# A layer of attention and sixteen experts on one core: five engine programs written anew

## The chip, the cores and the metric

The kernel runs on one core of one Trainium2 chip. TensorE (PE) multiplies, VectorE (DVE), ScalarE (ACT) and GpSimd (POOL) work elementwise, and SyncE (SP) issues the transfers; each follows a program of its own, and they wait for one another on semaphores. The metric is the time of one execution on the device, in microseconds (us); less is better.

## The reference

x has 16 batches of 512 tokens by 256 features, and each batch goes through one layer. What is computed, for a batch:

```
xn  = layernorm(x)
q, gates = split(xn @ Wqg);  k, v = split(xn @ Wkv)     # 16 heads: 16 key and 64 value features each
q, k, v  = q/|q|, k/|k|, v/|v|                          # per head and token
A   = square(relu(q @ k.T)) @ v                         # per head, 512 x 512, no softmax
att = tanh(|A|) * A/|A| * tanh(silu(gates))  @ Wout
s   = sigmoid(xn @ router.T)                            # 16 experts: best 2 of 4 groups, best 4 of their
c   = 2.5 * s / sum(s of the chosen), 0 elsewhere       # experts by s + bias
ffn = sum_e c[:, e] * (silu(xn @ gate_e.T) * (xn @ up_e.T)) @ down_e.T  +  two shared experts without c
out = x + att + ffn
```

## The kernel before

Every product that has to be exact is made of float16 halves: an operand is split into a high and a low part (`xh`, `xl`; `hh`, `hl`; `ah`, `al`), and a product is high x high, high x low and low x high, two PE instructions of 512 columns each for the 256 features. A projection of 128 features for all tokens, or an output block, is so a group of 6 instructions. The square of relu and v stay in float32.

The batches run in one loop: the first and the last are written out, 14 pass through a loop with a branch back on every engine. Within a batch PE follows one list, made by `pe_order()` and `plan_steps()`. Its main part are 32 **attention steps** (`STEPS`): in step s PE makes the values of a square that is ready ("AV", `values`, L1139, 4 float32 instructions of 512 columns) and two score tiles (`scores`, L1125, into two banks `sim`); ACT takes relu into a `ring` of squares, and the square is taken by ACT for the even tiles and by DVE for the odd ones (L883, L580). Between the steps stand the items of the 18 experts, each of which the plan gives a place: "g" (gate product), "u" (up), "d" (down, into `acc0`, `acc1`), "c" (the expert's row of combine weights, spread over 128 partitions by PE with a 0/1 matrix `sel16`, L1158), and the head sums ("N", L1147), tokens turned ("X") and router ("R") of the next batch. g, u, c and N write into three banks `wk0`, `wk1`, `wk2` in turn, and the bank of an item comes from the list. One semaphore, `work_full`, counts all items.

For an expert ACT makes `sg` = sigmoid-weighted gate (L889), DVE multiplies it by the combine row (L587) and by the up product (L599, `hf`), ACT and POOL split `hf` into `hh` and `hl` (L895, L1023), and PE makes the down product.

Q and K come token by token: for 128 tokens PE makes a row of q and k for all heads; DVE takes their norms by Newton steps and scales, ACT and POOL split them, and PE turns them with 64 transposes ("T", L1107) into `qt`, `kt`. V is made the same way at the start of the batch's body, 8 groups of 6: ACT squares it from the bank (L824) and copies it to `v_sb`, DVE sums the squares (L468) and scales it.

The end of the batch is the **output stage**: for each pair of heads t (8 of them) "G" is the gate product, "WB" spreads the head scales of the pair over the partitions (L1189, `wt` x `sel16`), DVE multiplies the gate by them (L631) and the values `agg` by that (`gated2`, L637), ACT and POOL split the result (`ah` L927, `al` L1039), and "O" (`output`) is the output product, 6 instructions into `acc0` and `acc1`. The x of the batch is added last, and SP stores `y_sb` to `out_t` (L383).

## Time and profile before

| | us |
|---|---|
| median of 3 runs (lowest, highest) | 3101.16 (3097.78, 3107.34) |
| the profiled execution's own time | 3102.68 |
| its span in the trace | 3100.9 |
| TensorE busy | 2869.5 (93%) |
| ScalarE, VectorE busy | 1980.7 (64%), 1821.8 (59%) |
| GpSimd busy | 737.2 (24%) |

The time is one run of the whole program; the span is what the profiler saw of it from the first to the last instruction, and the shares are parts of the span. Only busy time of PE is near the span, so the rows that matter are those of PE and of what it waits for, and the times of single operations on the other engines.

### The profile page before, as it was taken

Reading aid. Unit: us, or ns where it says so; the run is one execution under the profiler, and the core shown is the slowest. Engines: PE = TensorE matmul, PEld = TensorE weight load, DVE = VectorE, ACT = ScalarE, POOL = GpSimd, SP = SyncE. Lnnn points to the kernel's source line nnn. Section 1 sums busy time; section 2 is a strip of 40 time slices with the busy share of each in tenths; the row PEclk is TensorE's granted clock in tenths of the full one; section 3 lists DMA queues with packets and bytes.
Section 4 is the critical chain, followed back from the end, with each engine's and each line's share of the span. In section 5 each row is a group of like instructions: output and inputs, shape, how many; then the busy total and the mean of one; then the engine's idle time right before and its main releaser. Section 6 shows DMA issues by size and latency. Waiting matters only on the chain. (4 is left out here: it accounts for less than half of the span.)

```text
span 3100.9 us, 48985 instructions
## 1 busy us (share of the span) xinstructions
PE 2869.5 (93%) x14144; PEld 1159.8 (37%) x14144; DVE 1821.8 (59%) x3671; ACT 1980.7 (64%) x3498; POOL 737.2 (24%) x555
## 2 busy tenths in 40 slices
PE   1999999989899898998989999899998999989999
PEld 1343433333333333333433334333333334333433
DVE  8757456564565646556465565655656556564654
ACT  3766656667566675756657566665766756666665
POOL 0213122221322213122131221312223122221312
PEclk8999999999999999999999999999999999999999
DMA  3000000000000000000000000000000000000000
GB/s 152 11 1 22 1 22 1 1 22 1 22 1 1 22 1 22 1 1 22 1 22 1 22 2 1 22 1 22 1 1 22 1 22 1 1 22 1 14 1 8
DMA packets 19468, 39.95 MB, mean 13 GB/s; under 512 B 1584, under 2 KB 9904, under 8 KB 18128
## 3 DMA queue, kind: packets, MB, share of 16 engines
q1 hardware_dynamic: 19152, 36.11, 3.4%
q8 instruction: 152, 2.49, 0.3%
q14 instruction: 164, 1.34, 0.2%
HBM read 27.72 MB, written 8.39 MB: 12 GB/s over the span
## 5 line engine op out<-in xcount | busy, mean ns | idle before, releaser
L1023 POOL TENSOR_TENSOR hl<-hf,hh 128x512 f16<-128x512 f32 x288 | 403.1, 1400 | 1741.0 <-ACT hh L895 1741.0
L879 ACT ACTIVATE ring<-sim 128x512 f32<-128x512 f32 x1024 | 555.1, 596 | 382.7 <-PE sim L1125 376.1
L580 DVE TENSOR_TENSOR ring<-ring 128x512 f32<-128x512 f32 x512 | 379.1, 741 | 353.7 <-ACT ring L879 353.4
L1139 PE MATMUL av<-ring,v_sb 128*64 128x512 f32 x2048 | 548.8, 617 | 0.0
L599 DVE SCALAR_TENSOR_TENSOR hf<-wk,up_routed,sg 128x512 f32<-128x512 f32 x256 | 192.2, 751 | 229.9 <-PE wk L1066 220.1
L883 ACT ACTIVATE ring<-ring 128x512 f32<-128x512 f32 x512 | 325.2, 635 | 0.0
L587 DVE TENSOR_TENSOR sg<-sg,wk 128x512 f32<-128x512 f32 x256 | 176.0, 687 | 170.3 <-ACT sg L889 170.3
L1066 PE MATMUL wk<-wa_h,xh 128*128 128x512 f16 x384 | 129.6, 423 | 133.3 <-issue 74.7
L1066 PE MATMUL acc<-hh,down_h 128*128 128x512 f16 x576 | 225.0, 391 | 0.0
L1066 PE MATMUL acc<-hh,down_l 128*128 128x512 f16 x576 | 223.5, 388 | 0.0
L1066 PE MATMUL acc<-hl,down_h 128*128 128x512 f16 x576 | 222.9, 387 | 0.0
L824 ACT ACTIVATE sq<-wk 128x512 f32<-128x512 f32 x192 | 114.3, 596 | 165.4 <-PE wk L1066 158.6
L1039 POOL TENSOR_TENSOR al<-agg,ah 128x512 f16<-128x512 f32 x128 | 163.3, 1281 | 212.6 <-ACT ah L927 212.6
L889 ACT ACTIVATE sg<-wk,inv_m 128x512 f32<-128x512 f32 x288 | 198.4, 689 | 19.9 <-PE wk L1066 6.5
L1125 PE MATMUL sim<-qt,kt 64*128 64x512 f16 x1024 | 201.3, 387 | 0.5 <-DVE qt L509 0.5
L1125 PEld LDWEIGHTS sim<-qt,kt 64*128 64x128 f16 x1024 | 50.4, 92 | 400.6 <-issue 387.3
L895 ACT ACTIVATE hh<-hf 128x512 f16<-128x512 f32 x288 | 181.1, 629 | 0.0
L1066 PE MATMUL wk<-xh,up_h 128*128 128x512 f16 x576 | 174.0, 384 | 7.6 <-ACT v_sb L832 5.6
L1066 PE MATMUL wk<-xh,gate_h 128*128 128x512 f16 x576 | 174.2, 384 | 3.9 <-DVE hf L599 3.7
L919 ACT ACTIVATE gate_sb<-wk,inv_a 128x512 f32<-128x512 f32 x128 | 87.7, 685 | 137.9 <-PE wk L1066 137.9
L631 DVE TENSOR_TENSOR gate_sb<-gate_sb,wk 128x512 f32<-128x512 f32 x128 | 87.8, 686 | 147.3 <-PE wk L1189 147.3
L1066 PE MATMUL wk<-xh,gate_l 128*128 128x512 f16 x576 | 171.3, 379 | 0.0
(185 smaller groups left out, 4793.4 us busy)
## 6 DMA issues: line engine op xcount, KB each, us to landing
x_sb<-x SPq DMA_DIRECT2D x16, 512.0 KB, 4.8
y_sb<-x_t SPq DMA_DIRECT2D x16, 512.0 KB, 4.4
out_t<-y_sb SPq DMA_DIRECT2D x16, 512.0 KB, 3.2
raw_wa<-wa SPq DMA_DIRECT2D x1, 2560.0 KB, 9.2
raw_gate<-w_gate SPq DMA_DIRECT2D x1, 2304.0 KB, 14.4
raw_up<-w_up SPq DMA_DIRECT2D x1, 2304.0 KB, 19.4
raw_down<-w_down SPq DMA_DIRECT2D x1, 2304.0 KB, 24.4
raw_wo<-w_out SPq DMA_DIRECT2D x1, 1024.0 KB, 26.2
```

Of the source, the lines that this page charges most:

```text
L580: v.tensor_tensor(tile, tile, tile, ALU.mult).then_inc(square_odd, 1)
L587: v.tensor_tensor(sg[:, n % 2, :], sg[:, n % 2, :], bank(b, ("c", e))[:, :], ALU.mult).then_inc(sgc_done, 1)
L599: ins = v.scalar_tensor_tensor(out=hf[:, n % 2, :], in0=bank(b, ("u", e))[:, :], scalar=(up_routed if e < E else up_shared)[:, 0:1], in1=s ...
L879: a(ring[:, n % NR_, :], sim[n % 2][:, :], ACT.Relu, scale=S_SCALE).then_inc(relu_done, 1)
L883: a(ring[:, n % NR_, :], ring[:, n % NR_, :], ACT.Square).then_inc(square_even, 1)
L889: ins = a(sg[:, n % 2, :], bank(b, ("g", e))[:, :], ACT.Silu, scale=inv_m[:, 0:1])
L895: a(hh[:, n % 2, :], hf[:, n % 2, :], ACT.Copy).then_inc(h_hi, 1)
L1023: tt(hl[:, n % 2, :], hf[:, n % 2, :], hh[:, n % 2, :], ALU.subtract).then_inc(h_lo, 1)
L1039: tt(al[:, t % 2, :], agg[:, t, :], ah[:, t % 2, :], ALU.subtract).then_inc(a_lo, 1)
L1066: ins = mm(dst, w[k], xx[k], start=first and i == 0, stop=last and i == n - 1)
L1125: mm(sim[half][:, :], kt[rows, pair, j * P:(j + 1) * P], qt[rows, pair, :], start=True, stop=True).then_inc(sim_full, 1)
L1139: ins = mm(av[64 * half:64 * half + 64, :], v_sb[:, j, h * DV:(h + 1) * DV], ring[:, (2 * s + half) % NR_, :], start=(j == 0), stop=(j == ...
```

## The change

All five programs are written anew; what is computed, and the split into halves, stays.

- **Rounds.** The list is gone. A round i of the body holds on PE: gate(i) into a bank `wk`, down(i-1), up(i) into the same `wk`, then N, X or R where they are due, then the values of two steps and the scores of two steps, into four banks `sim0` to `sim3`. There are 16 rounds, and experts 16 and 17 (the shared ones) follow.
- **Squares.** All are taken by DVE, four per round.
- **Combine rows and head scales by DMA.** PE no longer spreads them: ACT copies the 16 rows from a bank, SP stores them in DRAM (`comb_rows`, `head_rows`) and loads each back into one of 4 slots of `comb`, repeated over the partitions. The multiplications read `comb`.
- **Q and K weight-stationary.** The weights are the stationary operand, so that PE makes q and k already turned, four groups (QK0 to QK3, `queries_keys`) for the next batch; ACT and DVE split them into `qk_st`, SP stores them in DRAM (`qk_rows`) and loads them with 16 transfers of 16 partitions into `qt` and `kt`. The norms come as sums over features (PE, `qk_sums`, 4 x 4 instructions with a 0/1 matrix `sel8`) and enter with the scales afterwards; the 64 transposes are gone.
- **The tail.** The next batch's Q, K and V are made at the end of this batch's body: after gates 0 to 7, down(16) and down(17) come QK0 to QK3 with their sums, V0, V1, and then for each t output(t) and V(t+2); after t = 2 the combine rows of the next batch (`combine_rows`).
- **Semaphores.** Each kind of item has its own.

Two attention steps of PE in the program before, in the middle of the first batch's list:

```order
L1139 MATMUL av<-ring,v_sb 64x512 x2
L1125 MATMUL sim0<-qt,kt 128x512
L1125 MATMUL sim1<-qt,kt 128x512
L1158 MATMUL wk2<-ct,sel16 64x512 x2
L1066 MATMUL wk0<-xh,gate_h 128x512 x2
L1066 MATMUL wk0<-xh,gate_l 128x512 x2
L1066 MATMUL wk0<-xl,gate_h 128x512 x2
L1139 MATMUL av<-ring,v_sb 64x512 x2
```

and one round of the program after, from its second gate row on (`wk` is the one bank of gate and up; `sim1` to `sim3` follow):

```order
L848 MATMUL wk<-xl,gate_h 128x512 x2
L848 MATMUL acc0<-hh,down_h 128x512
L848 MATMUL acc0<-hh,down_l 128x512
L848 MATMUL acc0<-hl,down_h 128x512
L848 MATMUL acc1<-hh,down_h 128x512
L848 MATMUL acc1<-hh,down_l 128x512
L848 MATMUL acc1<-hl,down_h 128x512
L848 MATMUL wk<-xh,up_h 128x512 x2
L848 MATMUL wk<-xh,up_l 128x512 x2
L848 MATMUL wk<-xl,up_h 128x512 x2
L937 MATMUL av<-ring,v_sb 64x512 x4
L922 MATMUL sim0<-qt,kt 128x512
```

The broadcast of the combine row is gone, the values of two steps and the scores of two steps stand together, and down lies between gate and up.

PE in the output stage before (`wk2` at the top is a gate product of a later t):

```order
L1066 MATMUL wk2<-xh,wa_h 128x512 x2
L1066 MATMUL wk2<-xh,wa_l 128x512 x2
L1066 MATMUL wk2<-xl,wa_h 128x512 x2
L1189 MATMUL wk0<-wt,sel16 128x512
L1066 MATMUL acc0<-ah,wo_h 128x512
L1066 MATMUL acc0<-ah,wo_l 128x512
L1066 MATMUL acc0<-al,wo_h 128x512
L1066 MATMUL acc1<-ah,wo_h 128x512
L1066 MATMUL acc1<-ah,wo_l 128x512
L1066 MATMUL acc1<-al,wo_h 128x512
L1066 MATMUL wk1<-xh,wa_h 128x512 x2
```

and after, where `wa_h` and `wa_l` with `xh` and `xl` into `sim1` are V(2) of the next batch:

```order
L848 MATMUL acc0<-ah,wo_h 128x512
L848 MATMUL acc0<-ah,wo_l 128x512
L848 MATMUL acc0<-al,wo_h 128x512
L848 MATMUL acc1<-ah,wo_h 128x512
L848 MATMUL acc1<-ah,wo_l 128x512
L848 MATMUL acc1<-al,wo_h 128x512
L848 MATMUL sim1<-wa_h,xh 128x512 x2
L848 MATMUL sim1<-wa_h,xl 128x512 x2
L848 MATMUL sim1<-wa_l,xh 128x512 x2
L848 MATMUL acc0<-ah,wo_h 128x512
```

Between two outputs stood a gate product and the spread of head scales; now a V product of the next batch stands there.

DVE ahead of and in the output stage before (the last expert products and head scales, `wst`, then two t):

```order
L587 TENSOR_TENSOR sg<-sg,wk1 128x512
L621 SCALAR_TENSOR_TENSOR an_a<-vn_t,an_y 128x64
L623 CAST wst<-an_a 128x4x16
L624 TENSOR_TENSOR wst<-an_a,wst 128x4x16
L599 SCALAR_TENSOR_TENSOR hf<-wk0,up_routed,sg 128x512
L631 TENSOR_TENSOR gate_sb<-gate_sb,wk0 128x512
L637 SCALAR_TENSOR_TENSOR agg<-agg,attn_scale,gate_sb 128x512
L631 TENSOR_TENSOR gate_sb<-gate_sb,wk1 128x512
```

and after, where `xl` are the low parts of the tokens, `qk_st` those of q and k, `vn_a<-sq` the sum of squares of a V product and `qn_a` the norms of q and k, all of the next batch:

```order
L347 TENSOR_TENSOR xl<-xf,xh 128x1024
L352 SCALAR_TENSOR_TENSOR qk_st<-wk,qk_st 128x512
L352 SCALAR_TENSOR_TENSOR qk_st<-sim0,qk_st 128x512
L352 SCALAR_TENSOR_TENSOR qk_st<-sim1,qk_st 128x512
L352 SCALAR_TENSOR_TENSOR qk_st<-sim2,qk_st 128x512
L367 TENSOR_REDUCE vn_a<-sq 128x8
L359 TENSOR_SCALAR qn_a<-sim3,eps_qkv 128x128
L361 RECIPROCAL qn_a<-qn_a 128x128
L499 TENSOR_TENSOR ring<-ring,comb 128x512
L504 SCALAR_TENSOR_TENSOR agg<-agg,attn_scale,ring 128x512
L367 TENSOR_REDUCE vn_a<-sq 128x8
```

The value sums of the next batch now stand between the products of one t and those of the next one, and the first of them ahead of t = 0.

SP's new transfers, the tail order of PE, DVE and ACT, and PE's products:

```diff
+            def keep_combine(b):
+                sp.wait_ge(ct_done, upto(b, 1, 1))
+                sp.dma_start(comb_rows, ct[:, :]).then_inc(combine_kept, 16)
+
+            def load_combine(b, e):
+                if e == 0:
+                    sp.wait_ge(combine_kept, upto(b, 16, 16))
+                elif e >= NC_:
+                    sp.wait_ge(sgc_done, upto(b, E, e - NC_ + 1))
+                sp.dma_start(comb[:, e % NC_, :], comb_rows[e:e + 1, :].to_broadcast([P, T])).then_inc(
+                    comb_loaded[e % NC_], 16)
+
+            def load_heads(b, t):
+                if t == 0:
+                    sp.wait_ge(heads_kept, upto(b, 16, 16))
+                elif t >= NC_:
+                    sp.wait_ge(gw_done, upto(b, NP_, t - NC_ + 1))
+                rows = head_rows[2 * t:2 * t + 2, :].unsqueeze(1).to_broadcast([2, DV, T])
+                sp.dma_start(comb[:, t % NC_, :], rows).then_inc(comb_loaded[t % NC_], 16)
+
+            def keep_qk(b):
+                for n in range(NQ):
+                    sp.wait_ge(qk_lo, upto(b, NQ, n + 1))
+                    sp.dma_start(qk_rows[:, n * P:(n + 1) * P, :].rearrange("c p t -> p c t"),
+                                 qk_st[:, n, :, :]).then_inc(qk_kept, 16)
+
+            def load_qk(b):
+
+                sp.wait_ge(qk_kept, upto(b, 16 * NQ, 16 * NQ))
+                for base, dst in ((0, qt), (H * DK, kt)):
...
                 sp.dma_start(y_sb[:, :, :], x_t[b].rearrange("(m p) t -> p m t", p=P)).then_inc(res_loaded, 16)
+                for e in range(E):
+                    load_combine(b, e)
+                sp.wait_ge(wt_done, upto(b, 1, 1))
+                sp.dma_start(head_rows, wt[:, :]).then_inc(heads_kept, 16)
+                for t in range(NP_):
+                    load_heads(b, t)
+                if not last:
+                    keep_qk(b + 1)
+                    load_qk(b + 1)
+                    keep_combine(b + 1)
...
+                for i in range(ROUNDS + 1):
+                    for n in (4 * i - 4, 4 * i - 3):
+                        if i:
+                            square(b, n)
+                    if i < ROUNDS:
+                        weigh(b, i)
+                    for n in (4 * i - 2, 4 * i - 1):
+                        if i:
+                            square(b, n)
+                    if i in [sums_at(t) for t in range(NP_ - 1)]:
+                        head_norms(b, (i - 4) // 2)
+                    hidden(b, i)
                     if not last:
...
+                    for _ in next_route:
+                        pass
+                    tokens_lo(b + 1)
+                    for n in range(NQ):
+                        lower_qk(b + 1, n)
+                    value_sums(b + 1, 0)
+                    qk_scales(b + 1)
                 for t in range(NP_):
                     gated(b, t)
                     gated2(b, t)
-                    if t == NP_ - 2 and not last:
-                        tokens_lo(b + 1)
-                    if t == NP_ - 1 and not last:
-                        sums(b + 1, 0)
-                        sums(b + 1, 1)
+                    if t + 1 < 2 * NB and not last:
+                        value_sums(b + 1, t + 1)
+                if not last:
+                    value_scales(b + 1)
                 finish(b)
+                if not last:
+                    for m in range(NB):
+                        unit_v(b + 1, m)
...
+                    for n in range(NQ):
+                        upper_qk(b + 1, n)
+                    raw_values(b + 1, 0)
+                for t in range(NP_):
+                    attention_hi(b, t)
+                    if not last:
+                        if t + 1 < 2 * NB:
+                            raw_values(b + 1, t + 1)
+                        if t == 2:
+                            combine_copy(b + 1)
...
+                ins.then_inc(wt_full, 1)
+
+            def queries_keys(b, n):
+                pe.wait_ge(xh_done, upto(b, 1, 1))
+                pe.wait_ge(xl_done, upto(b, 1, 1))
+                pe.wait_ge(gsilu_done, upto(b - 1, NP_, NB + n + 1))
+                weights_first(turns[n][:, :], wa_h, wa_l, slice(n * P, (n + 1) * P)).then_inc(qk_full, 1)
+
+            def qk_sums(b, n):
+                pe.wait_ge(qk_sq, upto(b, NQ, n + 1))
+                if n == 0:
+                    pe.wait_ge(wt_done, upto(b - 1, 1, 1))
+                for k in range(NB):
+                    at = 2 * H * k + 8 * n
+                    ins = mm(side[:, at:at + 8], sq[:, n % 2, k * P:(k + 1) * P], sel8[:, :], start=True, stop=True)
+                ins.then_inc(qn_full, 1)
+
+            def project_values(b, m):
+                half, k = m // NB, m % NB
+                if m < NB:
+                    pe.wait_ge(qk_lo, upto(b, NQ, m + 1))
+                    pe.wait_ge(qk_sq, upto(b, NQ, m + 1))
+                else:
+                    pe.wait_ge(raw_done, upto(b, 2 * NB, m - NB + 1))
+                blk, cols = slice(k * P, (k + 1) * P), slice(V_AT + half * T, V_AT + half * T + T)
+                products(turns[m % 4][:, :], ([xh[:, i, blk] for i in range(KD)], [xl[:, i, blk] for i in range(KD)]),
+                         ([wa_h[:, i, cols] for i in range(KD)],
...
+                for i in range(ROUNDS):
+                    pe.wait_ge(*((hf_done, upto(b, EA, i)) if i else (raw_done, upto(b, 2 * NB, NB + 1))))
+                    gate_up(b, "g", i, wk)
+                    if i:
+                        down(b, i - 1)
+                    pe.wait_ge(silu_done, upto(b, EA, i + 1))
+                    gate_up(b, "u", i, wk)
+                    if i in [sums_at(t) for t in range(NP_ - 2)]:
+                        pe.wait_ge(relu_done, upto(b, TILES, 4 * i))
+                        head_sums(b, (i - 4) // 2)
+                    if not last:
+                        for n in range(2):
...
+                    gates(b, t)
+                    if t == WT_AFTER:
+                        head_rows_of(b)
+                down(b, E)
+                down(b, E + 1)
+                if not last:
+                    for n in range(NQ):
+                        queries_keys(b + 1, n)
+                        if n:
+                            qk_sums(b + 1, n - 1)
+                    project_values(b + 1, 0)
+                    qk_sums(b + 1, NQ - 1)
+                    project_values(b + 1, 1)
+                for t in range(NP_):
+                    output(b, t)
+                    if not last:
+                        if t + 2 < 2 * NB:
+                            project_values(b + 1, t + 2)
+                        if t == 2:
+                            pe.wait_ge(qn_step, upto(b + 1, QN_STEPS, 1))
+                            combine_rows(b + 1)
```

## Rows read from the trace of the kernel before

**Rows 1.** The page: busy time of each engine.

```profile
PE 2869.5 (93%) x14144; PEld 1159.8 (37%) x14144; DVE 1821.8 (59%) x3671; ACT 1980.7 (64%) x3498; POOL 737.2 (24%) x555
```

**Rows 2.** Instructions on tile y_sb: issue, busy, first and last start.

```profile
L383 SPq DMA_DIRECT2D out_t<-y_sb x16: 388/395/402, 260.2 to 3097.7; - x16
...
L383 SPq MOVE out_t<-y_sb x14: 29/29/29, 263.9 to 2732.8; - x14
```

**Rows 3.** Timeline of PE, attention steps of batch 7: start, duration, instruction.

```profile
1498.93 0.40 PE L1158 MATMUL wk<-ct,sel 32*64 32x512 f16 x2
...
1499.26 0.60 PE L1066 MATMUL wk<-xh,gate_h 128*128 128x512 f16 x2
...
1500.66 1.08 PE L1139 MATMUL av<-ring,v_sb 128*64 128x512 f32 x4
...
1501.67 0.39 PE L1125 MATMUL sim<-qt,kt 64*128 64x512 f16 x2
...
1501.99 0.60 PE L1066 MATMUL wk<-xh,up_h 128*128 128x512 f16 x2
...
1503.30 0.95 PE L1147 MATMUL wk<-pair_sel,sq 128*128 128x2 f32 x8
...
1504.18 1.08 PE L1139 MATMUL av<-ring,v_sb 128*64 128x512 f32 x4
...
1541.35 1.94 PE L1139 MATMUL av<-ring,v_sb 128*64 128x512 f32 x8
...
1543.22 0.60 PE L1066 MATMUL wk<-xh,wa_h 128*128 128x512 f16 x2
```

**Rows 4.** Timeline of PE at the batch turn; in brackets the idle time before.

```profile
1566.22 0.38 PE L1189 MATMUL wk<-wt,sel 32*128 32x512 f16 x1
...
1566.54 0.39 PE L1066 MATMUL acc<-ah,wo_h 128*128 128x512 f16 x1
...
1592.55 1.01 PE L1066 MATMUL wk<-wa_h,xh 128*128 128x512 f16 x2 [5.18 <-issue]
...
1607.49 0.61 PE L1107 MATMUL wk<-id,qst 128*128 128x128 f16 x8
...
1607.93 0.61 PE L1107 MATMUL wk<-id,kst 128*128 128x128 f16 x8
...
1618.35 0.75 PE L1107 MATMUL wk<-id,qst 128*128 128x128 f16 x8 [2.88 <-DVE qt L509]
```

**Rows 5.** Windows: busy time of each engine, then TensorE's granted clock (0.57), DMA share.

```profile
1618.30:1622.30 4.00, 3.95 (x22) 2.16 (x22) 4.00 (x7) 1.02 (x1) 0.00 (x0) 0.57 0.02 4
```

**Rows 6.** Lines by form, whole trace: busy us, mean ns, idle before and its releaser.

```profile
L927 ACT ACTIVATE ah<-agg 128x512 f16<-128x512 f32 x128 | 80.3, 628 | 99.1 <-DVE agg L637 99.1
...
L1039 POOL TENSOR_TENSOR al<-agg,ah 128x512 f16<-128x512 f32 x128 | 163.3, 1281 | 212.6 <-ACT ah L927 212.6
...
L1023 POOL TENSOR_TENSOR hl<-hf,hh 128x512 f16<-128x512 f32 x288 | 403.1, 1400 | 1741.0 <-ACT hh L895 1741.0
...
L824 ACT ACTIVATE sq<-wk 128x512 f32<-128x512 f32 x192 | 114.3, 596 | 165.4 <-PE wk L1066 158.6 <-DVE wo_l L687 4.5 <-DVE vn_a L468 0.7
...
L468 DVE TENSOR_REDUCE vn_a<-sq 128x8 f32<-128x512 f32 x128 | 86.9, 679 | 103.9 <-ACT sq L824 103.6
...
L580 DVE TENSOR_TENSOR ring<-ring 128x512 f32<-128x512 f32 x512 | 379.1, 741 | 353.7 <-ACT ring L879 353.4
...
L637 DVE SCALAR_TENSOR_TENSOR agg<-agg,attn_scale,gate_sb 128x512 f32<-128x512 f32 x128 | 113.0, 883 | 4.5
...
L458 DVE TENSOR_TENSOR xl<-xf,xh 128x1024 f16<-128x1024 f32 x16 | 19.6, 1225 | 8.1 <-ACT xh L809 8.1
...
L889 ACT ACTIVATE sg<-wk,inv_m 128x512 f32<-128x512 f32 x288 | 198.4, 689 | 19.9 <-PE wk L1066 6.5
```

**Rows 7.** The page: DMA queue totals and the issue of the stores (us to landing).

```profile
q1 hardware_dynamic: 19152, 36.11, 3.4%
...
out_t<-y_sb SPq DMA_DIRECT2D x16, 512.0 KB, 3.2
```

More of the change, by code:

```diff
@@ L149, in work_order @@
[L149 to L166 removed]
+TILES = 2 * STEPS
@@ L892, in hidden_hi @@
+            def silu(b, e):
+                act.wait_ge(g_full, upto(b, EA, e + 1))
+                act.wait_ge(hf_done, upto(b, EA, e - 1))
+                g = wk if e < E else turns[2 * (e - E)]
+                a(sg[:, e % 2, :], g[:, :], ACT.Silu, scale=inv_m[:, 0:1]).then_inc(silu_done, 1)
             def hidden_hi(b, n):
@@ L1179, in gates @@
[L1179 to L1190 removed]
+                ins.then_inc(n_full, 1)
@@ new lines, in gate_up, with down @@
+            def gate_up(b, kind, n, bank):
+                wh, wl, full = (gate_h, gate_l, g_full) if kind == "g" else (up_h, up_l, u_full)
+                weights_first(bank[:, :], wh, wl, slice(n * P, (n + 1) * P)).then_inc(full, 1)
+            def down(b, n):
+                pe.wait_ge(h_hi, upto(b, EA, n + 1))
+                pe.wait_ge(h_lo, upto(b, EA, n + 1))
+                if n == 0:
+                    pe.wait_ge(y_done, upto(b, KD, 0))
+                for m in range(KD):
+                    mc = slice(m * P, (m + 1) * P)
+                    ins = products(acc[m][:, :], ([down_h[:, n, mc]], [down_l[:, n, mc]]),
+                                   ([hh[:, n % 2, :]], [hl[:, n % 2, :]]), first=(n == 0), last=False)
+                ins.then_inc(down_done, 1)
@@ L1212, in _ @@
             pe.wait_ge(set_done, 4)
-            for kind, n in FIRST:
-                if (kind, n) == ("QK", 0):
-                    pe.wait_ge(lo_done, len(cuts["wa"]))
-                ahead(0, kind, n)
+            turn_tokens(0, 0)
+            turn_tokens(0, 1)
+            router(0)
+            pe.wait_ge(lo_done, len(cuts["wa"]))
+            for n in range(NQ):
+                queries_keys(0, n)
+                if n == 0:
+                    pe.wait_ge(score_done, 1)
+                if n:
+                    qk_sums(0, n - 1)
@@ new lines, in free @@
+                def free(n):
+                    i = n // 4
+                    if n < 3:
+                        return [(raw_done, upto(b, 2 * NB, NB + 2 + n))]
+                    if n == 3:
+                        return [(ct_done, upto(b, 1, 1))]
+                    found = [(relu_done, upto(b, TILES, n - 3))]
+                    if n % 4 == 3 and i in [sums_at(t) for t in range(NP_ - 2)]:
+                        found.append((n_done, upto(b, NP_, (i - 4) // 2 + 1)))
+                    if not last and n in (4 * X_AT[0] + 2, 4 * X_AT[1] + 3):
+                        found.append((xf_done, upto(b + 1, 2, n % 4 - 1)))
+                    if not last and n == 4 * R_AT + 3:
+                        found.append((score_done, upto(b + 1, 1, 1)))
+                    return found
@@ L1245, in _ @@
+                for t in range(NP_):
+                    output(b, t)
+                    if not last:
+                        if t + 2 < 2 * NB:
[3 more added lines that the diff above has]
+                            combine_rows(b + 1)
             rounds(pe, body)
```

946 lines of the change are left out of this document (329 added, 617 removed).

## Prediction

> **What bounds the kernel now.** I read the page's busy times first: PE is busy for 93% of the span, the next engine for 64% [rows 1]. So each microsecond that the change takes from PE's stream counts, and each wait that it puts into that stream counts as well. Next, the stores: they give one batch. The reader should see that the issue in the loop comes 14 times between 263.9 and 2732.8, so that 13 periods take 2468.9 and one takes 189.9 [rows 2]. Last, PE's timeline: the attention steps follow one another with no idle mark [rows 3], and what PE loses in a period lies at the batch turn. There it stands still for 5.18 when the loop branches back, and for 2.88 when the first transposes wait for DVE's `qt` [rows 4]; after the second of these a window of 4.00 ran at a granted clock of 0.57 of full speed [rows 5], near the lower of its two levels (1.2 GHz of 2.4).
>
> **What the change removes from PE, per batch.** Durations are differences of starts.
>
> 16 broadcasts of combine rows at 1499.26 - 1498.93 = 0.33 [rows 3]: 5.3.
>
> 64 transposes, 8 groups at 0.44 [rows 4]: 3.5.
>
> 8 spreads of head scales at 0.32 [rows 4]: 2.6.
>
> The values of two steps together: one step takes 1.01, two in a row 1.87 [rows 3], so 0.15 less for each of 16 rounds: 2.4.
>
> A gate product ahead of float32 values took 1.40, an up product ahead of head sums 1.31 [rows 3]. I read the 0.09 as the cost of the change of type. Half of the changes go, 16 in and 16 out; the way back I take at the same size. 2.9 together (bounds 0 and 2.9).
>
> That is 16.7. **What it adds on PE:** four `qk_sums`, each of the form of the head sums, 0.88 [rows 3]: 3.5. The turns of combine and head rows are now float32, 4 instructions each; the trace has none, and the bounds are the 0.33 of two float16 ones and the 0.88 of the head sums [rows 3]; I take 0.55 each, 1.1. Q, K and V cost the same groups of six as before. So PE's work falls by 16.7 - 4.6 = 12.1.
>
> **What it removes in waits:** the wait for `qt`, 2.88 [rows 4], and its window at low clock, 4.00 x 0.43 = 1.7 [rows 5]: 4.6. The stop at the branch stays: all engines still branch, and nothing else is named there than "issue". In total 16.7 of gain a batch.
>
> **Costed at nothing: the rounds.** `wk` now holds gate(i), then up(i). ACT must have read the gate, 0.69 [rows 6], before up starts; down, six products at 1.31 as the up shows [rows 3], stands between and hides it. Without that cover it would be 0.7 on each of 16 rounds. A round is 3 x 1.31 + 1.87, two pairs of scores at 1501.99 - 1501.67 = 0.32 [rows 3] and two changes of type: 6.6 of PE. DVE has four squares at 0.741 in it, and two products with a bank or a row, which I take at no more than 0.74 as well, 4.4 together [rows 6], and the rest of the next batch's norms and routing; so DVE has about two to spare. The values wait for squares made while gate, down and up run, 4.0.
>
> The Trainium skill would count this otherwise: "Perfetto Trace Analysis", section "Optimizing Tensor Performance" (Matmuls), wants independent groups of products to rotate through different PSUM banks, so that reading one overlaps the next one's products. Gate and up share a bank here, which speaks against the change; by that rule 0.7 is exposed in 16 rounds of 16 batches, and the sum would be 180 higher. The cover of 1.31 by down is longer than the reading, so I keep nothing for all rounds but the first.
>
> **The waits that it adds, per batch.**
>
> Round 0 has no down between gate and up: 0.69 [rows 6] and a remainder of 0.1 ahead of gate(1), since the scores of 0.64 cover most of `hf`. 0.8 (bounds 0 and 1.5). In round 1 down(0) waits for `hh` and `hl` behind gate(1), 0.63 (as `ah`) + 1.40 less 1.31: 0.7 [rows 6].
>
> QK0 needs `xl` of the next batch, 1.225 on DVE [rows 6], and DVE comes to it only after the last expert's product and the head scales, ACT to `xh` only after its gates. Two downs, 2.6, cover part. I take 2.0 (bounds 0 and 4).
>
> The first output. After V0, DVE does value sums and the scales of q and k ahead of the first `gated`; all of the chain follows V0: square 0.60, sums 0.68, two small operations 0.6, `gated` 0.74 (as a square), `gated2` 0.88, `ah` 0.63, `al` 1.28 [rows 6], 5.4, and seven hand-overs, for which I take 0.5 (bounds 0 and 1). PE has V1 and a `qk_sums` to do meanwhile, 2.2. 3.7 (bounds 2 and 5).
>
> The outputs after it, the largest term. DVE has value sums(t+1) between `gated2(t)` and `gated(t+1)`; they wait for ACT's square(t+1), which stands behind `ah(t)`. So from one `gated2` to the next: 0.63 + 0.60 + 0.68 + 0.74 + 0.88 = 3.5 [rows 6], 3.7 with hand-overs. Seen from PE, output(t), V(t+2), square, sums, both products, `ah` and `al` make a loop over two outputs of 1.3 + 1.3 + 4.8 = 7.4, 7.6 with hand-overs, against 5.2 of PE's own work. Output(7) starts 3 x 7.6 + 3.7 = 26.5 after output(0); PE's work there is 7 outputs, 6 V groups and one turn, 17.8: 8.7 of waits. At t = 2 ACT copies the combine rows before `ah(3)`, and PE makes them after output(2) and V(4): 1.28 + 1.3 + 1.3 + 0.6 + a copy of 0.6 [rows 6], 5.7 with hand-overs, where 3.1 were due: 2.7. Together 11.4 (bounds 6 and 13; the lower end when DVE's two products run without POOL beside them).
>
> Low clock. Two of these waits (2.0, 3.7) are about as long as the 2.88 that has a low-clock window behind it [rows 4, 5]; 1.7 each, 3.4 (bounds 0, and 7 if the outputs bring more).
>
> Sum of waits: 0.8 + 0.7 + 2.0 + 3.7 + 11.4 + 3.4 = 22.0. Net 22.0 - 16.7 = +5.3 a batch, for the 15 tails that make a next batch: +80. The last batch keeps the gain alone, -12. The prologue has q and k go out and come back once, two transfers one behind the other; the store lands after 3.2 [rows 7], so about +6 (bounds 0 and 20). The profiled execution's 3102.7 plus 74 is 3177, and I forecast **3180**. (That execution lies 1.5 above the median of the runs.)
>
> **Transfers, where nothing here shows the new shapes.** SP's list is in order: 16 combine loads, head rows, 8 loads of 256 KB, then the stores and loads of q and k. A load over all engines: the queue moved 36.11 MB in 3.4% of 16 x 3100.9, so 21.4 KB per us and engine [rows 7], and 256 KB take 0.75; the 2 MB of q and k 6.1. Those of q and k are issued once `gated(4)` is done; three outputs and the sums of y follow, over 10, before scores need them. I take nothing on the path.
>
> **Rivals.**
>
> *The head-scale loads use few engines* (chance 0.27). Their source is two rows, each repeated 64 times. If the two rows go to two engines, a load takes 128 / 21.4 = 6.0 [rows 7], longer than the 3.7 between outputs, and eight in a row take 48. The last `gated` is then some 4 late, and q and k land behind them, up to 5 late: 4 to 9 in 15 batches, and the last batch, with nothing else in its output stage, loses 48 less some 17 of work under it, 31. 60 + 31 to 135 + 31 more: 3271 to 3346. For it: the form with two outer rows. Against it: a transfer that is cut by partition, as the store may be, goes to all. By the Trainium skill, "DMA: Bandwidth & Descriptors", section "Why a DMA increments its semaphore by 16 and not by 1", the number of engines is the largest up to 16 that divides the outermost dimension of both sides, which would be two here; no run here shows it yet.
>
> *PE stays fed at the turn* (0.16), the other side. The 5.18 [rows 4] at the branch ends when PE has its next instructions; with other waits just ahead of the branch, PE's queue may be filled while it waits, and 5.2 and a low-clock stretch of the size above, 1.7, go: 6.9 a batch. It decides from 5.6 a batch on (78 / 14). 3180 - 14 x 6.9 = 3083, and with the outputs at their lower bound, 5.4 less a batch, 3008. Against it: the branch is still there.
>
> *The sums cancel* (0.08): waits at 17 a batch, 3092 to 3112.
>
> *DVE becomes the bound of the rounds* (0.05). All squares are on it, and a square may stretch beside POOL's `hl`; 0.5 a round would be 7.5 to 8 a batch, 3300.
>
> **How the numbers follow.** The forecast's own case, 3130 to 3235, has 0.36; 3112 to 3130, where the outputs stand at their lower bound, 0.08. With the rivals that is 1. Runs of before lie 9.6 apart, 0.3%, which is what I call the same. Faster than that needs the second rival, 0.16; same 0.08; slower the rest, 0.76. The range, 3090 to 3330, leaves out the deeper part of the second rival and the upper end of the first.
>
> **What would show it.** Right: rounds with PE unbroken at 6.6; outputs 3.7 apart with V between, waits of PE at `al`, DVE waiting for `sq` of V ahead of `gated`; a longer wait at t = 3; no T, c or WB. Wrong: outputs 2.6 to 3.0 apart; PE waiting for `comb` through DVE, or for `qt` and `kt` at the head of the batch (the first rival); no stop at the branch (the second); PE waiting for `ring` in the rounds (the fourth); `xl` waits beyond 4.

## The result and the profile after

The change makes the kernel slower: 3326.18 us median (3320.91 to 3332.28) against 3100.76, a ratio of 1.0725 with an interval of 1.0699 to 1.075. The forecast of 3180 had the direction, and 3326 lies within its range, but the loss is 225 where 79 were forecast. The profiled execution has a span of 3330.3.

The page of the kernel after, busy times and the queue, which answer to [rows 1] and [rows 7]:

```profile
PE 2763.9 (83%) x13120; PEld 1181.9 (35%) x13120; DVE 1988.4 (60%) x3893; ACT 1591.5 (48%) x2778; POOL 499.4 (15%) x427
...
q1 hardware_dynamic: 127904, 188.10, 22.7%
```

PE's busy time fell by 105.6, 6.6 a batch, although its mean granted clock fell too, from 0.976 to 0.922; the span rose by 229. So PE waits, and more of its work runs at the lower clock. The queue moves five times the bytes, and its share rose from 3.4% to 22.7%. The stores of the first two and the last two batches, which answer to [rows 2], first of the kernel after, then two of the kernel before:

```profile
300.62 0.41 SPq L272 DMA_DIRECT2D out_t<-y_sb  x1
...
499.74 0.42 SPq L272 DMA_DIRECT2D out_t<-y_sb  x1
...
3132.99 0.41 SPq L272 DMA_DIRECT2D out_t<-y_sb  x1
...
3327.13 0.39 SPq L272 DMA_DIRECT2D out_t<-y_sb  x1
```

```profile
442.46 0.40 SPq L383 DMA_DIRECT2D out_t<-y_sb  x1
...
2919.77 0.40 SPq L383 DMA_DIRECT2D out_t<-y_sb  x1
```

From the second store to the last but one there are thirteen periods in either kernel: 202.6 each instead of 190.6, 12.0 more, 156 together. (The 189.9 of the prediction has the first batch of the loop in it, which takes 182.3.) The rest stands at the ends: the first store comes at 300.6 instead of 260.2, 40 more; the batch behind it takes 17 more, and the last one 194 instead of 178, 16 more. Together that is the 229.

The records of instructions and of the granted clock split these 12.0. In a period before, PE was idle for 11.1, and for 8.0 of its busy time the clock was at the lower of its two levels (1.2 of 2.4 GHz), which costs it half of that, 4.0 (a pair of instructions of one form took 0.86 at that level, at 1480.12, and 0.43 at the full clock, at 1484.03). After, it is idle for 30.4, and 19.3 of its busy time is at the lower level, which costs 9.6. So its work, put at the full clock, fell by 12.9, its idle time rose by 19.3, and the lower clock takes 5.6 more. (An estimate, since the ends of matmuls are modelled.)

PE's timeline at the turn of one batch in the middle of the run, which answers to [rows 4] (start, duration, instruction, idle time before it and its releaser):

```profile
1461.92 0.59 PE L848 MATMUL wk<-xh,wa_h 128*128 128x512 f16 x2 [1.27 <-issue]
...
1477.61 0.58 PE L848 MATMUL acc<-ah,wo_h 128*128 128x512 f16 x1 [4.31 <-POOL al L821]
...
1487.67 0.38 PE L848 MATMUL acc<-ah,wo_h 128*128 128x512 f16 x1 [2.19 <-POOL al L821]
...
1494.00 0.38 PE L848 MATMUL acc<-ah,wo_h 128*128 128x512 f16 x1 [2.60 <-POOL al L821]
...
1509.07 0.38 PE L848 MATMUL acc<-ah,wo_h 128*128 128x512 f16 x1 [2.83 <-POOL al L821]
...
1510.64 1.06 PE L848 MATMUL wk<-xh,gate_h 128*128 128x512 f16 x2
...
1514.26 0.60 PE L848 MATMUL wk<-xh,up_h 128*128 128x512 f16 x2 [0.86 <-ACT sg L707]
...
1522.92 1.14 PE L922 MATMUL sim<-qt,kt 64*128 64x512 f16 x4 [7.20 <-DMA kt<-qk_rows]
...
1531.21 1.03 PE L848 MATMUL wk<-xh,gate_h 128*128 128x512 f16 x2 [7.14 <-DVE hf L465]
...
1538.95 0.60 PE L848 MATMUL wk<-xh,gate_h 128*128 128x512 f16 x2
...
1545.35 0.60 PE L848 MATMUL wk<-xh,gate_h 128*128 128x512 f16 x2
```

The reader sees three things. The waits for `al` in the output stage were forecast: from 1511 to 1713, one period, the view of waits gives 14.4 of them. A round, 1538.95 to 1545.35, is 6.4 with nothing in brackets. And between them stand two waits that the forecast did not have, 7.20 for `kt` and 7.14 for `hf`.

Not every turn looks like this one. Of the 15 turns, 7 have the wait for `kt`, 3.0 to 7.2. At 7 others ACT stands still at its branch, with no wait that the trace names ("issue"), and PE waits 3.4 to 7.0 for its `sg` (ACT's eighth such stop falls on a turn with a wait for `kt`); at one more, PE itself stands still for 12.81. The wait for `hf` stands at 14 of the 15, 4.1 to 8.5. ACT's such waits over the whole trace (total, times, longest), one of these turns, and PE's own stop:

```profile
ACT sg L707 <- issue: 74.4, 8, 10.4
```

```profile
1319.35 0.69 ACT L707 ACTIVATE sg<-wk,inv_m 128x512 f32<-128x512 f32 x1 [10.41 <-issue]
```

```profile
713.56 1.03 PE L848 MATMUL wk<-xh,gate_h 128*128 128x512 f16 x2 [12.81 <-issue]
...
1320.09 1.04 PE L848 MATMUL wk<-xh,up_h 128*128 128x512 f16 x2 [7.03 <-ACT sg L707]
```

SP's issues at the turn of 1510 tell what the two waits shown first hang on (here the duration spans the instructions of a group, waits between them included):

```profile
1488.13 0.49 SPq L224 DMA_DIRECT2D comb<-head_rows  x1
1488.75 8.23 SPq L229 DMA_DIRECT2D qk_rows<-qk_st  x4
1504.21 4.50 SPq L241 DMA_DIRECT2D qt<-qk_rows  x8
1508.75 4.09 SPq L241 DMA_DIRECT2D kt<-qk_rows  x8
1512.95 0.35 SPq L208 DMA_DIRECT2D comb_rows<-ct  x1
...
1524.13 0.37 SPq L260 DMA_DIRECT2D y_sb<-x_t  x1
1524.62 17.94 SPq L215 DMA_DIRECT2D comb<-comb_rows  x7
```

The stores of q and k start when the last head-scale load is out, and take 8.2 to issue. The loads start when the stores have landed, at 1504, and PE gets `kt` at 1522.9. The combine rows are stored behind them, the y rows loaded behind the stored y, and the first combine load goes out at 1524.6; `hf` needs it, and gate(1) needs `hf`.

In the last batch, which loads no q and k, the head scales are alone. Two of DVE's eight products of gate and head scale there, and the window of that stretch (busy times of PE, PEld, DVE, ACT, POOL; granted clock; DMA share):

```profile
3286.88 0.69 DVE L499 TENSOR_TENSOR ring<-ring,comb 128x512 f32<-128x512 f32 x1 [3.84 <-DMA comb<-head_rows]
...
3292.23 0.69 DVE L499 TENSOR_TENSOR ring<-ring,comb 128x512 f32<-128x512 f32 x1 [3.87 <-DMA comb<-head_rows]
```

```profile
3273.70:3315.00 41.30, 18.90 (x57) 5.86 (x54) 9.55 (x14) 6.84 (x11) 6.91 (x6) 0.72 0.13 47
```

They are 5.35 apart, each waiting for its load, with a DMA share of 0.13. That is what two of 16 engines busy would give, and so 128 KB / 5.35 = 24 KB per us for each.

### The profile page after: what moved, and what is told of

It reads as the page before. It is cut to its first block, busy times and chain, and to the rows that moved or that the text cites. A ratio compares the mean times of both kernels' runs of the same rounds, so it can differ in the third digit from the quotient of the medians.

```text
span 3330.3 us, 46023 instructions
## 1 busy us (share of the span) xinstructions
PE 2763.9 (83%) x13120; PEld 1181.9 (35%) x13120; DVE 1988.4 (60%) x3893; ACT 1591.5 (48%) x2778; POOL 499.4 (15%) x427
## 3 DMA queue, kind: packets, MB, share of 16 engines
q1 hardware_dynamic: 127904, 188.10, 22.7%
## 4 chain that ended last, share of the span: by engine, by line
PE 51%; issue 27%; DMA 7%; DVE 5%; ACT 4%; POOL 3%; SPq 3%; POOLq 0%; ACTq 0%; DVEq 0%
PE wk L848 16%; PE av L937 11%; PE acc L848 9%; PE sim L848 6%; DMA out_t<-y_sb 4%; PE sim L922 3%; PE sim L944 3%; DMA comb<-comb_rows 2%; POOL hl L817 2%; POOL al L821 1%; DMA qk_rows<-qk_st 1%; PE sim L898 1%; ACT ring L736 1%; SPq L241 1%; SPq L229 1%
## 5 line engine op out<-in xcount | busy, mean ns | idle before, releaser
L448 DVE TENSOR_TENSOR ring<-ring 128x512 f32<-128x512 f32 x1024 | 693.7, 711 | 279.6 <-ACT ring L701 265.3
L817 POOL TENSOR_TENSOR hl<-hf,hh 128x512 f16<-128x512 f32 x288 | 344.1, 1195 | 1913.2 <-ACT hh L712 1857.3
L454 DVE TENSOR_TENSOR sg<-sg,comb 128x512 f32<-128x512 f32 x256 | 176.9, 691 | 245.3 <-DMA comb<-comb_rows 202.1
L848 PE MATMUL acc<-ah,wo_h 128*128 128x512 f16 x256 | 115.7, 452 | 245.1 <-POOL al L821 245.1
L367 DVE TENSOR_REDUCE vn_a<-sq 128x8 f32<-128x512 f32 x128 | 87.8, 686 | 307.5 <-ACT sq L679 307.5
L848 PE MATMUL wk<-xh,gate_h 128*128 128x512 f16 x544 | 175.5, 406 | 109.5 <-DVE hf L465 96.7
L465 DVE SCALAR_TENSOR_TENSOR hf<-wk,up_scale,sg 128x512 f32<-128x512 f32 x256 | 192.1, 750 | 30.2 <-issue 14.2
L848 PE MATMUL wk<-xh,up_h 128*128 128x512 f16 x512 | 157.2, 390 | 53.9 <-ACT sg L707 53.9
L937 PEld LDWEIGHTS av<-ring,v_sb 128*64 128x64 f32 x2048 | 122.8, 136 | 204.3 <-issue 143.3
L743 ACT ACTIVATE ah<-agg 128x512 f16<-128x512 f32 x128 | 80.6, 629 | 236.8 <-DVE agg L504 236.8
L848 PE MATMUL wk<-xl,gate_h 128*128 128x512 f16 x544 | 173.4, 402 | 0.0
L848 PE MATMUL wk<-xl,up_h 128*128 128x512 f16 x512 | 156.0, 387 | 0.0
```

Of the source, the lines that this page charges most:

```text
L448: tt(tile, tile, tile, ALU.mult).then_inc(square_done, 1)
L454: tt(sg[:, e % 2, :], sg[:, e % 2, :], comb[:, e % NC_, :], ALU.mult).then_inc(sgc_done, 1)
L465: v.scalar_tensor_tensor(out=hf[:, e % 2, :], in0=up[:, :], scalar=up_scale[:, 0:1], in1=sg[:, e % 2, :], op0=ALU.mult, op1=ALU.mult).then ...
L817: tt(hl[:, n % 2, :], hf[:, n % 2, :], hh[:, n % 2, :], ALU.subtract).then_inc(h_lo, 1)
L848: ins = mm(dst, w[k], xx[k], start=first and i == 0, stop=last and i == n - 1)
L937: ins = mm(av[64 * half:64 * half + 64, :], v_sb[:, j, h * DV:(h + 1) * DV], ring[:, (2 * s + half) % NR_, :], start=(j == 0), stop=(j == ...
```

## The experiments

Theory A: the new waits come from SP's list, in which stores, loads and combine rows stand one behind the other. Theory B: they come from the head-scale loads, which occupy two engines and hold what is issued behind them. A third question was whether DVE's order sets the pace of the outputs. Each of the first four runs changes one thing in the kernel after (3326).

**Stores of q and k early (e1).**

```diff
                 for t in range(NP_):
+                    if t == NC_ and not last:
+                        keep_qk(b + 1)
                     load_heads(b, t)
                 if not last:
-                    keep_qk(b + 1)
                     load_qk(b + 1)
```

> Only SP's list is changed: the four stores of q and k stand between the head-scale loads of t = 3 and t = 4, no longer behind all eight; their loads stay behind the eighth. Theory A (the waits of PE for kt, 7.2 a batch, and for hf behind the combine row, 7.1, come from SP's list, in which stores, loads and combine rows stand one behind the other): the loads of q and k start some 14 earlier, the kt wait goes and part of the hf wait with it, 10 to 14 less a batch, 3130 to 3190. Theory B (the head-scale loads, which move over two engines, hold the queue, so stores issued among them land no earlier): at most 3 less a batch, 3280 to 3326.

Measured: 3336.65 (1.0755, 1.0737 to 1.0773), no gain. SP's issues:

```profile
1465.82 8.98 SPq L229 DMA_DIRECT2D qk_rows<-qk_st  x4
1474.94 14.65 SPq L224 DMA_DIRECT2D comb<-head_rows  x4
1489.73 14.18 SPq L241 DMA_DIRECT2D qt<-qk_rows  x8
1503.96 8.77 SPq L241 DMA_DIRECT2D kt<-qk_rows  x8
```

The wait for `kt` did go in the loop, but the last output of the batch now waits 9.85 for `al`:

```profile
1516.45 0.58 PE L849 MATMUL acc<-ah,wo_h 128*128 128x512 f16 x1 [9.85 <-POOL al L822]
```

The stores take 9 to issue here as well, and the loads of q and k now 23 instead of 8.6. Over the whole trace PE's waits for `kt`, for `sg` and under "issue" fell by 87, and those for `al` grew by 91: this change of order only chose who waits. For the stores theory A fails; the time lies somewhat above B's range too, but no gain is what B says.

**Combine rows early (e2).** The store of the rows ahead of the loads of q and k, and four combine loads behind those.

```diff
             load_qk(0)
+            for e in range(NC_):
+                load_combine(0, e)
...
-                for e in range(E):
+                for e in range(NC_, E):
                     load_combine(b, e)
...
                     keep_qk(b + 1)
+                    keep_combine(b + 1)
                     load_qk(b + 1)
-                    keep_combine(b + 1)
+                    sp.wait_ge(gw_done, upto(b, NP_, NP_))
+                    for e in range(NC_):
+                        load_combine(b + 1, e)
```

> Only SP's list is changed: the store of the combine rows stands ahead of the loads of q and k, and the first four combine loads directly behind those loads, ahead of the load of y. Theory A: the wait of gate(1) for hf, 7.1, falls to 1 or 2, the kt wait stays at 7 or grows by 2: 3 to 6 less a batch, 3240 to 3285. Rival (the combine loads land only when all of q and k has landed, whatever their place): less than 2 a batch, above 3296.

Measured: 3274.64 (1.0546, 1.0523 to 1.0568), as theory A had it. PE's waits over the whole trace (total, times, longest):

```profile
PE sim L927 <- DMA kt<-qk_rows: 60.9, 8, 15.4
PE wk L853 <- ACT sg L712: 60.6, 31, 8.1
...
PE wk L853 <- DVE hf L470: 14.3, 14, 2.3
```

The wait for `hf` fell from 96.7 to 14.3: it was SP's order, a part that theory A had right. That for ACT's `sg`, 53.9 in the kernel after, stays at 60.6, and ACT stands still at 8 turns here too.

**Head scales in two loads of one row each (e3).**

```diff
-                rows = head_rows[2 * t:2 * t + 2, :].unsqueeze(1).to_broadcast([2, DV, T])
-                sp.dma_start(comb[:, t % NC_, :], rows).then_inc(comb_loaded[t % NC_], 16)
+                for h in range(2):
+                    row = head_rows[2 * t + h:2 * t + h + 1, :].to_broadcast([DV, T])
+                    sp.dma_start(comb[DV * h:DV * h + DV, t % NC_, :], row).then_inc(comb_loaded[t % NC_], 16)
```

The two counts that wait for `comb_loaded` follow.

> Only the head-scale loads are changed: two transfers of one row to 64 partitions each in place of one of two rows, so that the source no longer has two outer rows. Theory B: a load takes about 1 instead of 5.35, the stores of q and k behind them are issued in 0.6 each instead of 2 and land earlier, the kt wait falls by 4 or more; the last batch loses its waits for head scales, some 20: 3235 to 3265. Theory A: only the last batch gains, 20, and SP's eight more issues cost nothing: 3300 to 3310.

Measured: 3221.81 (1.0369, 1.0324 to 1.0413), 104 less, more than theory B asked for and far from A's 20. SP's issues and PE's wait at the turn:

```profile
1453.86 2.15 SPq L230 DMA_DIRECT2D qk_rows<-qk_st  x4
1458.85 3.65 SPq L242 DMA_DIRECT2D qt<-qk_rows  x8
```

```profile
1493.18 1.03 PE L849 MATMUL wk<-xh,gate_h 128*128 128x512 f16 x2 [6.61 <-DVE hf L466]
```

The stores go out in 2.15 instead of 8.23 and land 3.1 after their issue, by the median. No wait for `kt` is left in the loop, ACT no longer stands still at the branch, and PE's waits for `sg` fell from 53.9 to 19.1; the waits for `al` (14.4 in the batch) and for `hf` (6.6) stay. So both kinds of turn hung on the two-row loads. A period, store to store, fell from 202.6 to 197.5.

**Value sums one place later (e4).**

```diff
-                    value_sums(b + 1, 0)
-                    qk_scales(b + 1)
                 for t in range(NP_):
                     gated(b, t)
                     gated2(b, t)
-                    if t + 1 < 2 * NB and not last:
-                        value_sums(b + 1, t + 1)
+                    if not last:
+                        value_sums(b + 1, t)
+                        if t == 0:
+                            qk_scales(b + 1)
```

> Only DVE's list is changed: the value sums of the next batch stand one place later, so that the two products of t and t+1 no longer wait for V(t+1) and its square; the scales of q and k stand behind t = 0. Theory of the output loop (value sums between the products set the pace, 14.4 of PE's waits for al): 8 to 11 less a batch, 3165 to 3210. Theory B: the head-scale loads, 8 x 5.35 = 43 from their first issue on, become the pace, 3 to 5 less a batch, 3250 to 3285. The kt wait does not fall in either.

Measured: 3332.24 (1.0735, 1.0717 to 1.0753): nothing, less than either. DVE's products in the output stage show the reason:

```profile
1487.79 0.69 DVE L499 TENSOR_TENSOR ring<-ring,comb 128x512 f32<-128x512 f32 x1 [2.57 <-DMA comb<-head_rows]
1493.14 0.69 DVE L499 TENSOR_TENSOR ring<-ring,comb 128x512 f32<-128x512 f32 x1 [3.27 <-DMA comb<-head_rows]
1498.48 0.69 DVE L499 TENSOR_TENSOR ring<-ring,comb 128x512 f32<-128x512 f32 x1 [3.26 <-DMA comb<-head_rows]
```

5.35 apart again. With the sums out of the way the head-scale loads set the pace, and the wait for `kt` grew (9.8 at this turn). DVE's order (e3) and the loads (here) each make waits for `al` by themselves, and had covered each other. So the edits were put together.

**Two loads and early combine rows (e5)** (the third and the second diff):

> The two loads per t of e3_heads_two_loads (3222) and the early combine rows of e2_combine_early together. If the wait of gate(1) for hf, 6.6 a batch in e3, comes from the combine rows behind the stored y, it falls to 1 or less and takes its low clock with it: 6 to 7 less a batch, 3115 to 3135. Rival (the combine loads land behind the q and k loads all the same): 3190 or more.

Measured: 3133.20 (1.0101, 1.0084 to 1.0118), as expected; the waits for `hf` fell from 112.0 in e3 to 20.0.

**Two loads and later sums (e6)** (the third and the fourth diff):

> The two loads per t of e3_heads_two_loads and the later value sums of e4_sums_behind together. If the pace of the output stage was DVE's order, hidden in e4 behind the head-scale loads of 5.35, the waits for al fall from 14.4 to about 4, outputs 2.6 to 3 apart: 9 to 11 less a batch than e3, 3055 to 3090. Rival (ACT's copy of the combine rows at t = 2 and its own squares set the pace): no more than 4 less, 3160 or more.

Measured: 3061.12 (0.9874, 0.9858 to 0.9891), as expected in time: 161 less than the two loads alone, by an edit that alone gave nothing. PE's waits for `al` fell from 225.2 to 108.0, 6.8 in one batch where about 4 were expected; those for `sg` rose from 19.1 to 51.7, since ACT stands still at 11 turns again. The lower clock cost PE 77 less than in e3, by the same working as above.

**All three (e7):**

> All three edits: two loads per t, early combine rows, later value sums. If the three causes add up, 15 to 17 less a batch than e3_heads_two_loads: 2965 to 2995, below the kernel before. Rival (with a shorter output stage q and k land late again, kt wait of 3 to 6): 3030 to 3070.

Measured: 2986.82 (0.9634, 0.9618 to 0.965). The three edits add up to within 15 (104, 89 and 161 off 3326 would be 2972), and the kernel is faster than the one before.

**All three, and the copy of the combine rows at t = 3 (e8):**

```diff
-                        if t == 2:
+                        if t == 3:
                             combine_copy(b + 1)
```

> As e7_all_three, and ACT copies the combine rows of the next batch at t = 3 instead of t = 2, when PE has long made them, so that ah(3) does not wait behind the copy. The wait counted for it in the forecast was 2.7: 2 to 3 less a batch than e7, 2925 to 2960. Rival (by then PE has other work to do there): within 10 of e7.

Measured: 2975.26 (0.9597, 0.9581 to 0.9613), 12 less, where 30 to 45 were expected: a miss. The waits for `al` did fall by 44 in the trace (108.5 to 64.2), but that for `sg` rose by 31 (69.6 to 100.5). ACT's first instruction of the next round, in this kernel:

```profile
1556.76 0.69 ACT L713 ACTIVATE sg<-wk,inv_m 128x512 f32<-128x512 f32 x1 [11.42 <-issue]
```

ACT stands still for 11.42 at its branch, as it did at 8 turns of the kernel after; here it does so at 12:

```profile
ACT sg L713 <- issue: 132.4, 12, 11.6
```

It stands in a stretch in which the queues are full:

```profile
1546.00:1556.70 10.70, 2.75 (x12) 1.10 (x12) 6.70 (x17) 0.00 (x0) 0.59 (x1) 0.90 1.14 163
```

The DMA share is 1.14 (shares come from packets that overlap). The trace also holds the packets that bring instructions, as queues of their own (q8 and q14). At this turn one of q14 starts at 1548.4 and takes 1.04, the next one ends at 1555.2, and ACT starts 1.5 later. At all 12 such stops of e8 ACT starts 1.49 to 1.55 after a packet of q14 has ended, and at the 13 stops of PE at the branch in the kernel before, PE starts 1.25 to 1.51 after one of q8. So the stop ends when instructions have landed. Whether they are late because the queues are full is what the next run asks.

**Q between the head-scale loads (e9).** From the last kernel, SP's list alone; `load_qk` has a second argument now, 0 for q and 1 for k:

```diff
...
                 for t in range(NP_):
+                    if t == 4 and not last:
+                        keep_qk(b + 1)
+                    if t == 6 and not last:
+                        load_qk(b + 1, 0)
                     load_heads(b, t)
                 if not last:
-                    keep_qk(b + 1)
-                    keep_combine(b + 1)
-                    load_qk(b + 1)
+                    load_qk(b + 1, 1)
+                    keep_combine(b + 1)
```

> From e8_all_three_copy (2975), only SP's list: the stores of q and k go out behind the head-scale loads of t = 3, the eight loads of q between those of t = 5 and t = 6, the loads of k behind t = 7, the combine rows last. In e8 ScalarE does nothing for 11.4 at the branch, until the queues have landed q, k and the combine rows, and PE's first up product waits 8.0 for it. Theory (the instructions behind the branch come late because the queues are full of q and k): the transfers end some 6 earlier and so does the stop, 4 to 7 less a batch, 2880 to 2920. Rival (the stop belongs to the branch): 2960 to 2990. Should the loads of t = 6 and 7 land late behind q, the waits for al grow by 2 to 4 a batch.

Measured: 2903.96 (0.9362, 0.9347 to 0.9378), 71 less. ACT at the branch:

```profile
1516.97 0.69 ACT L717 ACTIVATE sg<-wk,inv_m 128x512 f32<-128x512 f32 x1 [4.26 <-PE wk L858]
```

Now it waits for PE, whose gate product is its input, and no "issue" of ACT above 2 is left at any turn; PE's waits for `sg` are back at 19.1. The branch is the same; the queues are not. In the stretch before it the DMA share is 0.33:

```profile
1512.60:1516.90 4.30, 2.90 (x13) 1.10 (x12) 3.85 (x14) 0.11 (x1) 1.17 (x1) 1.00 0.33 106
```

The two late loads of t = 6 and 7 cost nothing: the waits for `al` are 65.1.

**The first batch's q and k first (e10):**

```diff
-            keep_combine(0)
             sp.wait_ge(lo_done, len(pieces))
             load_qk(0, 0)
             load_qk(0, 1)
+            keep_combine(0)
```

> From e9_q_between_heads, only the prologue: the loads of q and k of the first batch stand ahead of the store of its combine rows, which waits for the router until 89, while the weights are ready at 76. If the wait for kt of 15 in the first batch is that order, the first store comes 8 to 14 earlier, and the time falls by as much against e9. Rival (the combine rows then are late in the place of q and k): within 5.

Measured: 2887.12 (0.9309, 0.9294 to 0.9325), 17 less, a little more than expected: the wait for `kt` in the prologue fell from 16.2 to 1.9. This is the fastest kernel of the study, 6.9% below the one before. By the working above, its span is 216 shorter, of which PE's work at full clock is 197; idle time is 14 longer, and the lower clock costs 33 less. What the change took from PE shows in the time once the transfers no longer stand in its way.

**The kernel before with late loads (e11):**

```diff
             def body(b, last):
+                sp.wait_ge(work_full, filled(b, ("V", 3)))
                 if not last:
                     load_x(b + 1)
```

> The kernel before, in which SP loads the next x and the y rows (512 KB each) only after V(3) of the batch, some 10 after the branch instead of at it; the store of the last batch's y stays at it. Theory (PE's stop of 5.18 at the branch is its instructions arriving late behind these transfers): the stop falls to 2 or 3, 2 to 4 less a batch with the low clock behind it, 3045 to 3075. Rival (the stop belongs to the branch): 3090 to 3110.

Measured: 3067.94 (0.9899, 0.9882 to 0.9915), in the theory's range of time; but the stop fell less than it said:

```profile
1575.17 1.01 PE L1067 MATMUL wk<-wa_h,xh 128*128 128x512 f16 x2 [4.38 <-issue]
```

4.38 at this turn against 5.18 in [rows 4], and 3.9 to 4.4 at all 13 against 5.0 to 5.9; PE's "issue" waits fell from 74.7 to 58.5 in all. The transfers had a part in the stop; most of it stays with the fetch of instructions that the branch asks for, or with the store of y that was left there. Of the 35 that the span lost, idle time is only 9. Most of the rest is the clock: at the lower level PE was busy for 110.5 before and for 51.2 here, which is 30 less. Before, a stretch of 6.8 at the lower level followed most of the stops, and one of 3.4 the wait for `qt` behind it; here a single stretch of 3.4 is left at a turn. The wait for `qt` is as long as in [rows 4], and behind it the granted clock is 1.00, where [rows 5] had 0.57:

```profile
1599.91 0.62 PE L1108 MATMUL wk<-id,qst 128*128 128x128 f16 x8 [2.88 <-DVE qt L510]
```

```profile
1600.50:1605.00 4.50, 4.33 (x28) 1.72 (x26) 4.50 (x8) 3.00 (x5) 0.00 (x0) 1.00 0.02 4
```

## Why the prediction was right in sign and too small

**What held.** PE's gains and the rounds. Its work at full clock fell by 12.9 a batch, forecast 12.1. Rounds take 6.4, forecast 6.6, with no wait but 0.3 here and there; gate and up in one bank cost nothing behind down, and round 0 waits 0.86 for `sg` where 0.8 were forecast. The rule of the Trainium skill's "Perfetto Trace Analysis", section "Optimizing Tensor Performance", on rotating banks, from which the forecast estimated 180 more, has no counterpart in this trace. All squares on DVE did not make it the bound. The output stage's waits for `al` are 14.4 in the batch, forecast 3.7 + 11.4. With the loads out of the way DVE's order alone makes 14.4 of them (e3), and taking it away gave 161 (e6); in the kernel after itself the head-scale loads would have made the outputs wait in any case (e4). QK0 waited 1.3, forecast 2.0, under the mark "issue" and not for `xl`.

**The step that failed** is the sentence on the transfers, "I take nothing on the path". It set 6.1 of moving against "over 10" of cover, and left out what lies around the moving: stores that must be queued, issued and landed before the first load goes out, 16 loads at 0.54 of issue each (the trace of before already had 0.4 for an issue, [rows 2]), and the combine rows last in SP's list, behind all of it and behind the stored y. At the turn shown it came to 7.2 for `kt` and 7.1 for `hf`. Over the 15 turns `kt` took 41.9, `hf` 92.6, the waits for `sg` 34.8 above the 19.1 that e3 has, and PE's own stop 12.8: 12.1 a turn. In the first batch `kt` and `hf` took 16.0 and 4.1, where 6 were allowed.

**A second term was too small:** the lower clock. The forecast had 3.4 for the new waits less 1.7 behind `qt`, so 1.7 more a batch; measured are 5.6 more. Its size was read from one window behind the wait of 2.88 for `qt`, and e11 shows that this wait by itself does not bring the lower clock.

**The first rival was the larger cause**, with 0.27 and 3271 to 3346. It named the place (two rows, two engines), the price (6.0 a load, measured 5.35) and the last batch (31 of extra waits less 12 of gain; that batch took 16 more than before). e3 shows it: the same bytes in loads of one row took 104 off. By the Trainium skill, "DMA: Bandwidth & Descriptors", section "Why a DMA increments its semaphore by 16 and not by 1", two engines were to be expected from an outermost dimension of two; the share of 0.13 agrees. The rival, too, had the path only in part: it saw q and k late by up to 5, and not that stores issued behind such loads cost SP 2 each instead of 0.5.

**The wait for the combine rows** was in no case of mine. e5 against e3 gives 89 for it, e2 against the kernel after 52.

**The stop at the branch** was kept at 5.2. In the kernel after PE has it at one turn alone, the 12.81 shown above; at the turn of 1510 gate(0) follows output(7) with no bracket. So the second rival's event occurred too, worth some 5 a batch on the other side, and was outweighed. Why PE is spared is not shown; the page counts fewer packets of q8, behind which PE's stops ended before (first the page of the kernel before, then of the kernel after):

```profile
q8 instruction: 152, 2.49, 0.3%
```

```profile
q8 instruction: 29, 0.48, 0.1%
```

The stop had not gone for good: at half of the turns ACT stands there instead, in this kernel already.

In sum, idle time was forecast to rise by 18.6 of new waits less 2.9 for `qt`, 15.7 a batch, and rose by 19.3: some 12 for the transfers, which were taken at nothing, less 5 for PE's stop, which was kept, with the other waits some 3 below their size (QK0 and `al` are 0.7 each of that; the rest was not taken apart). The lower clock took 5.6 where 1.7 were forecast, and work fell by 12.9 where 12.1 were. That makes the 12.0 against 5.3. The ends of the run, 73 more where 5 were forecast, make up the rest.

## What to carry to other kernels

Before a transfer is called hidden, write its whole chain with starting times: the event that lets it be queued, what stands ahead of it in the issuing engine's list, issue, landing, and the same again for the load that must wait for it. The repeated source whose outermost dimension is two moved here as over two engines, 5.35 for 256 KB; one transfer per row took 104 off the time. Read more than one turn of a loop: here half of them lost their time at another place than the one first read. When one edit gives nothing, look in its trace for the wait that took the place of the one removed, and try both together: here an edit that alone gave nothing was worth 161 beside another.

## What the runs showed of the hardware that was not expected

A store issued behind the two-row loads took longer to issue, not only to land: the four stores of q and k took 8.2 to issue behind the two-row loads and 2.15 behind one-row loads, and their landing fell from a median of 5.7 to 3.1. A small transfer behind large ones lands late: the 32 KB of `comb_rows` took a median of 11.0 in the kernel after, stored behind the loads of q and k, and 1.6 in e8, stored ahead of them; `head_rows`, of the same size, took 1.6 in both. And an engine that branches back while the queues are full can stand still with no named wait: ACT 11.4 in e8 at a DMA share of 1.14, nothing in e9 at 0.33. Such a stop ended 1.25 to 1.55 after a packet of instructions, at 12 turns of e8 and 13 of the kernel before. That these packets come late because they share the engines with the data fits e3, e8, e9 and e11; how much of the stop in the kernel before belongs to the branch itself stays open.
